# Cross-attention on one core: the next pair's queries and first keys ahead of the last product with the values, denominators and output moved later

## The reference

```python
# x: (2, 256, 256), ctx: (2, 4096, 256), 16 heads of 64
q = (layernorm(x) @ w_q); k = ctx @ w_k; v = ctx @ w_v      # split into heads
attn = softmax(q @ k^T * 64 ** -0.5)                          # (2, 16, 256, 4096)
x = x + (attn @ v, heads side by side) @ w_o
```

## Time and profile before

| | |
|---|---|
| median of 3 runs | 1456.81 us (1455.27 to 1457.78) |
| profiled execution | 1455.65 us |
| its span, first to last instruction | 1453.9 us, mean granted clock 0.964 |
| TensorE busy | 1299.6 us, 89% |
| VectorE busy | 983.6 us, 68% |
| ScalarE busy | 877.8 us, 60% |
| GpSimd busy | 245.4 us, 17% |
| first queries projected (L518) to last output (L606) | 25.8 to 1167.3 us |

### The profile page before, as it was taken

The page is one execution under the profiler, slowest core; times in us unless marked ns, Lnnn a source line. Parts: engine busy times, 40 slices in busy tenths (PEclk is TensorE's granted clock), DMA queues, the critical chain, the costliest instruction groups (busy, mean ns, idle before and its releaser), DMA issues. The chain is left out here.

```text
span 1453.9 us, 22869 instructions
## 1 busy us (share of the span) xinstructions
PE 1299.6 (89%) x8447; PEld 1003.3 (69%) x8447; DVE 983.6 (68%) x1256; ACT 877.8 (60%) x1562; POOL 245.4 (17%) x245
## 2 busy tenths in 40 slices
PE   4999999999999999899999999999999969887643
PEld 3877787868687878697768687877777733666322
DVE  4657676777767687656777767685858555735476
ACT  5758585857676676565767676675757412534152
POOL 4202021211212120111211212020303022020000
PEclk9999999999999999999999999999999979998776
DMA  4000000000000001200000000000000054261000
GB/s 163 1 1 19 1 19 9 12 19 1 19 1 15 1 19 55 80 1 13 7 19 1 20 1 19 1 20 1 15 1 5 1 169 64 27 80 16 22 0 15
DMA packets 29684, 34.70 MB, mean 24 GB/s; under 512 B 3984, under 2 KB 26000, under 8 KB 29328
## 3 DMA queue, kind: packets, MB, share of 16 engines
q1 hardware_dynamic: 27536, 29.83, 8.0%
q0 software_dynamic: 2048, 3.43, 1.7%
HBM read 25.89 MB, written 0.52 MB: 18 GB/s over the span
## 5 line engine op out<-in xcount | busy, mean ns | idle before, releaser
L463 DVE TENSOR_TENSOR prob_sum<-prob_sum,probs 128x1024 f32<-128x1024 f32 x224 | 264.5, 1222 | 164.6 <-ACT probs L382 163.9
L382 ACT ACTIVATE probs<-scores_a 128x1024 f32<-128x1024 f32 x128 | 131.2, 1025 | 209.1 <-PE scores_a L578 208.1
L315 POOL TENSOR_TENSOR k_split<-prob_sum,k_split 64x512 fp32r<-64x512 f32 x128 | 165.0, 1289 | 303.2 <-ACT prob_sum L358 303.2
L442 DVE TENSOR_REDUCE step_max<-scores_a 128x2 f32<-128x1024 f32 x128 | 156.9, 1225 | 37.3 <-PE scores_a L566 35.5
L442 DVE TENSOR_REDUCE step_max<-scores_b 128x2 f32<-128x1024 f32 x128 | 155.7, 1216 | 0.0
L577 PE MATMUL scores_a<-q_twice,k_split 128*128 128x256 f32 x512 | 139.1, 305 | 5.0 <-ACT q_low_max L373 4.9
L308 POOL TENSOR_TENSOR w_lo<-w_raw,w_hi 128x768 fp32r<-128x768 f32 x16 | 34.9, 2181 | 593.8 <-ACT w_hi L327 593.7
L382 ACT ACTIVATE probs<-scores_b 128x1024 f32<-128x1024 f32 x128 | 131.3, 1026 | 0.0
L577 PE MATMUL scores_b<-q_twice,k_split 128*128 128x256 f32 x512 | 128.4, 283 | 0.0
L578 PE MATMUL scores_b<-q_low_max,k_ones 128*128 128x256 f32 x512 | 127.9, 282 | 0.0
L578 PE MATMUL scores_a<-q_low_max,k_ones 128*128 128x256 f32 x512 | 127.9, 283 | 0.0
(11 more groups left out here) (214 smaller groups left out, 2641.3 us busy)
## 6 DMA issues: line engine op xcount, KB each, us to landing
ctx_rows<-in_ctx_dram SPq DMA_DIRECT2D x10, 512.0 KB, 3.6
w_raw<-in_L_xattn_w_v_dram SPq DMA_DIRECT2D x14, 256.0 KB, 3.2
probs<-in_ctx_dram SPq DMA_DIRECT2D x6, 512.0 KB, 6.1
grouped<-dots_sb SPq DMA_DIRECT2D x16, 136.0 KB
grouped<-dots_sb POOLq DMA_DIRECT2D x16, 136.0 KB, 13.2
w_raw<-in_L_xattn_w_q_dram SPq DMA_DIRECT2D x16, 128.0 KB, 2.3
w_raw<-in_L_xattn_w_k_dram SPq DMA_DIRECT2D x16, 128.0 KB, 2.4
wo_pair<-in_L_xattn_w_o_dram SPq DMA_DIRECT2D x16, 128.0 KB, 2.1
```

What stands on the lines that cost most here:

```text
L315: pool.tensor_tensor(k_split[0:DH, B, keys], k_staged_b[j % 2], k_split[DH:P, B, keys].bitcast(F32), ALU.subtract).then_inc(k_low[B], 1)
L382: act.activation(probs[:, j % 2, h, :], flat_scores[h], ACT.Exp, scale=SCALE).then_inc(exp_done, 1)
L442: dve.tensor_reduce(step_max[:, :, 1 - h, j - 1], scores[h][:, :, :], X, ALU.max).then_inc(max_done, 1)
L463: dve.tensor_tensor(prob_sum[:, h, :], prob_sum[:, h, :], probs[:, j % 2, h, :], ALU.add).then_inc(sum_done, 1)
```

## The change

The program of each engine keeps its operations but gets another order around the boundary of two pairs.

- TensorE: within a batch, `project_q` and `project_k` of step 0 of the *next* pair are issued before the last `product_with_v` of this one. In the next pair, `sum_over_keys` comes behind `project_k` of step 1, `project_output` behind the first `scores_for_max` at step 2. For the first pair of a batch `sum_over_keys` comes behind `project_k` of step 0.
- ScalarE: `split_weights` for the next pair behind the exponentials of step 3; the copies of the next queries and of the high keys of step 0 at the end of the pair; the staged copies of steps 0 and 1 wait for `den_made`.
- VectorE: `divide` moves behind the correction of keys 1 (L435 at j = 1), `add_output` from j = 1 to behind `low_queries` at j = 2.
- The hardware loop covers four pairs of a batch, not six; pairs 5 to 7 are written out.

```diff
@@ -215,11 +215,12 @@
 
 
             body(b * PAIRS, b, 0, 0)
-            with eng.Fori(0, PAIRS // 2 - 1) as k:
+            with eng.Fori(0, PAIRS // 2 - 2) as k:
                 for parity in (1, 0):
                     i = k * 2 + (2 - parity)
                     body(b * PAIRS + i, b, i, parity)
-            body((b + 1) * PAIRS - 1, b, PAIRS - 1, 1)
+            for i in range(PAIRS - 3, PAIRS):
+                body(b * PAIRS + i, b, i, i % 2)
 
         def context_banks(n):
 
@@ -247,6 +248,9 @@
 
         def is_first(it):
             return isinstance(it, int) and it == 0
+
+        def stays_in_batch(i):
+            return not (isinstance(i, int) and i == PAIRS - 1)
 
         def last_batch(b, i):
 
@@ -337,25 +341,38 @@
                     own = v_near[:, tiles, :] if half == parity else v_far[:, half, tiles, :]
                     act.activation(own, src[:, :, 0:PAIR], ACT.Copy).then_inc(v_copied, 1)
 
-            def body(it, b, i, parity):
-                if not is_first(it):
-                    split_weights(it, b, i)
-
+            def high_queries(it):
                 act.wait_ge(q_made, it + 1)
                 for h in (A, B):
                     for half in (0, DH):
                         act.activation(q_twice[half:half + DH, h, :], v_ps[h * DH:(h + 1) * DH, 0:SEQ],
                                        ACT.Copy).then_inc(q_high, 1)
+
+            def high_keys(it, j):
+                keys = slice(j * CHUNK, (j + 1) * CHUNK)
+                act.wait_ge(k_made, STEPS * it + j + 1)
+                ps = k_ps[j % 2]
+                act.activation(k_split[0:DH, A, keys], ps[0:DH, :], ACT.Copy).then_inc(k_high, 1)
+                act.activation(k_split[DH:P, B, keys], ps[DH:P, :], ACT.Copy).then_inc(k_high, 1)
+
+            def stage_keys(it, j):
+                if j >= 2:
+                    act.wait_ge(k_low[B], STEPS * it + j - 1)
+                else:
+                    wait_past(act, den_made, it)
+                act.activation(k_staged_b[j % 2], k_ps[j % 2][DH:P, :], ACT.Copy).then_inc(k_staged, 1)
+
+            def body(it, b, i, parity):
+                if is_first(i):
+                    if b > 0:
+                        split_weights(it, b, i)
+                    high_queries(it)
                 for j in range(STEPS + 1):
                     if j < STEPS:
                         keys = slice(j * CHUNK, (j + 1) * CHUNK)
-                        act.wait_ge(k_made, STEPS * it + j + 1)
-                        ps = k_ps[j % 2]
-                        act.activation(k_split[0:DH, A, keys], ps[0:DH, :], ACT.Copy).then_inc(k_high, 1)
-                        act.activation(k_split[DH:P, B, keys], ps[DH:P, :], ACT.Copy).then_inc(k_high, 1)
-                        if j >= 2:
-                            act.wait_ge(k_low[B], STEPS * it + j - 1)
-                        act.activation(k_staged_b[j % 2], ps[DH:P, :], ACT.Copy).then_inc(k_staged, 1)
+                        if j > 0 or is_first(i):
+                            high_keys(it, j)
+                        stage_keys(it, j)
                     if j > 0:
 
                         keys = slice((j - 1) * CHUNK, j * CHUNK)
@@ -383,8 +400,13 @@
                                        ).then_inc(exp_done, 1)
                     if j == 0:
                         copy_v(b, i, parity, STEPS - 1)
+                    if j == 3 and stays_in_batch(i):
+                        split_weights(it + 1, b, i + 1)
                     if next_group(b, i, j) is not None:
                         context_high(act, next_group(b, i, j))
+                if stays_in_batch(i):
+                    high_queries(it + 1)
+                    high_keys(it + 1, 0)
                 if next_group(b, i, STEPS) is not None:
                     context_high(act, next_group(b, i, STEPS))
             for b in range(BATCH):
@@ -424,8 +446,6 @@
                                       ALU.subtract).then_inc(q_low, 1)
                     dve.tensor_tensor(q_low_max[DH:P, B, :], v_ps[DH:P, 0:SEQ], q_twice[DH:P, B, :].bitcast(F32),
                                       ALU.subtract).then_inc(q_low, 1)
-                if not is_first(it):
-                    divide(it - 1)
                 for j in range(STEPS + 1):
                     if j < STEPS:
                         keys = slice(j * CHUNK, (j + 1) * CHUNK)
@@ -435,7 +455,7 @@
                         dve.tensor_tensor(k_split[DH:P, A, keys], ps[0:DH, :], k_split[0:DH, A, keys].bitcast(F32),
                                           ALU.subtract).then_inc(k_low[A], 1)
                     if j == 1 and not is_first(it):
-                        add_output(it - 1, last_batch(b, i))
+                        divide(it - 1)
                     if j > 0:
                         for h in (A, B):
                             dve.wait_ge(pre_made, 2 * (STEPS * it + j - 1) + h + 1)
@@ -443,6 +463,8 @@
                                               ).then_inc(max_done, 1)
                     if j == 2:
                         low_queries()
+                        if not is_first(it):
+                            add_output(it - 1, last_batch(b, i))
                 dve.wait_ge(max_done, 2 * STEPS * (it + 1))
                 dve.tensor_reduce(row_max[:, :, :], step_max[:, :, :, :], X, ALU.max).then_inc(max_chain, 1)
                 dve.wait_ge(max_chain, 2 * it + 1)
@@ -608,10 +630,8 @@
                 last.then_inc(y_made, 1)
 
             def body(it, b, i, parity):
-                project_q(it, b)
-                if not is_first(it):
-                    sum_over_keys(it - 1)
-                pe.wait_ge(w_low, it + 1)
+                if is_first(i):
+                    project_q(it, b)
                 for j in range(STEPS):
                     if j >= 2:
 
@@ -619,14 +639,20 @@
                         pe.wait_ge(k_staged, STEPS * it + j - 1)
                     if is_first(i):
 
+                        pe.wait_ge(w_low, it + 1)
                         pe.wait_ge(ctx_low, DC * (j + 1 if b == 0 else (b + 1) * LOADS))
-                    project_k(it, j)
-                    if j == 1 and not is_first(it):
-                        project_output(it - 1)
+                    if j > 0 or is_first(i):
+                        project_k(it, j)
+                    if j == (0 if is_first(i) else 1) and not is_first(it):
+                        sum_over_keys(it - 1)
                     if j == 2 and is_first(i):
                         pe.wait_ge(ctx_low, DC * (b + 1) * LOADS)
                     if j > 1:
+                        if j == 2:
+                            pe.wait_ge(q_high, 4 * it + 4)
                         scores_for_max(it, j - 2)
+                    if j == 2 and not is_first(it):
+                        project_output(it - 1)
                     if j > 3:
                         project_v(it, b, i, parity, j - 4)
                 scores_for_max(it, STEPS - 2)
@@ -657,6 +683,10 @@
                         product_with_v(it, b, i, parity, j - 1)
                     if next_group(b, i, j) is not None:
                         transpose_context(next_group(b, i, j))
+                if stays_in_batch(i):
+                    project_q(it + 1, b)
+                    pe.wait_ge(w_low, it + 2)
+                    project_k(it + 1, 0)
                 product_with_v(it, b, i, parity, STEPS - 1)
                 if next_group(b, i, STEPS) is not None:
                     transpose_context(next_group(b, i, STEPS))
```

## The result

| | before | changed |
|---|---|---|
| median of 4 runs | 1456.93 us | 1472.84 us (1472.3 to 1474.54) |
| profiled execution, its span | 1455.65, 1453.9 us | 1472.59, 1470.8 us |

The change makes the kernel slower: ratio 1.0113, 95% interval 1.0095 to 1.013. The spans differ by 16.9 us.

A forecast was written before the change was run, and what follows sets the result against it. A pair's end hangs on its first product for the values, behind VectorE's chain and the addition, despite TensorE's 89% busy. Ordinary boundaries 8.4, jumps 4.4, batch boundary 1.2: +14.0 on 1455.65, so 1470 us; range 1457 to 1477.

The forecast's parts named there:

- The chain: Pair boundary: denominators, staged copy, high keys 1, correction, division, first maximum, with the addition still to come before v(0).
- den_made later: Ordinary boundary: the denominators come 1.2 us later, behind the next pair's queries and keys on TensorE.
- First maximum: VectorE's first row maximum after an ordinary boundary starts at 460.65 instead of 460.88, 0.2 us sooner.
- v(0) and the ordinary boundary: First product for the values waits for the late output addition; net +0.7 us a boundary, bounds +0.4 to +1.1.
- Rule of v(0) plus a constant: A pair ends a constant time after its first product for the values, which hangs on VectorE's chain and y_added.
- The jump: Loop's jump back, one a batch, falls between product 7 and keys 1: +1.5 us each, bounds 0 and 2.2.
- Batch boundary: Pair 7 to 8: keys 0 ahead of the denominators make the first product for the values 1.2 us later.
- Exponentials: Stretch of exponentials: moving split_weights and w_lo there costs 0, at worst 1.5 us a pair.
- rival 3: Contention in the exponentials: w_lo's 1.5 us of blocking stops them, 21 us on top, 1491; chance 0.03.
- moved with w_lo: The fold ends some 1.5 us sooner, but that time goes to a running sum in e-step 3 or 4.
- Rival 1: TensorE is the bound and gets its idle time back at the fold: 21 us faster, 1435; chance 0.11.
- Rivals 2 and 4: First: late addition hidden, only jumps cost, 1457, chance 0.11. Second, counted within it: fold's wait and denominators swap places, 1456.

The follow-up runs named there:

- 2: Changed kernel with the division moved ahead of the correction of keys 1 on VectorE; 1452.83 us, ratio 0.9991.
- 3: Changed kernel with staged copies and reciprocal in columns of prob_sum that the denominators' product does not read; 1457.21 us, ratio 1.0015.
- experiment 1: Changed kernel with add_output ahead of low_queries at step 2 on VectorE; 1469.01 us, ratio 1.0106.
- experiment 7: Kernel before with only split_weights for the next pair moved behind the exponentials of step 3; 1439.58 us, ratio 0.9897.

## Why the prediction was right, point by point

- **Direction, mechanism and size.** Predicted 1470 and slower by 14 us, measured 1472.84 and slower by 15.9. That the two are so close is in part luck: the sum's own terms, the boundaries, came to 19.8 in the traces, and 2.9 us went off outside the pairs. The chain was the one described, and two experiments that break it at different links (2 and 3) each give 1.2 us a boundary back.
- **den_made later.** Predicted 1.2 us later than before, measured 1.49 (6.54 against 5.05). The rest lies in the rows between product 6 and the denominators (455.86 to 463.66 where written out): four blocks each 0.04 to 0.14 longer than booked, 0.3 in all. The prediction's bounds had such an amount, as switches between shapes; no run separates the cause.
- **First maximum.** Predicted 0.2 sooner, measured 0.14 in the loop and 0.0 where written out.
- **v(0) and the ordinary boundary.** Predicted +0.7 for both. Measured +0.85 at v(0) in the loop and +1.0 where written out, +0.8 in the mean of 12 periods.
- **Rule of v(0) plus a constant.** True for the change (v(0)→end 20.01 against 20.05), false as a rule: experiment 1. Removing y_added's wait brings v(0) 0.89 sooner and wins 0.25.
- **The jump.** This term was mis-sized: 1.5 each, measured 3.3 and 2.2 at the denominators, 7.4 in place of 4.4 in the sum. The price was taken from one jump of the kernel before, where TensorE waits 1.3 to 1.8 us at the four jumps; here it waits 2.10 and 2.17, and at one jump the clock fell on top. Why the wait is longer in the new order is open.
- **Batch boundary.** exp→v(0) +1.3, predicted +1.2; the period rose by 2.7, because the stretch of exponentials of pair 7 took 1.3 more. The stretch waits for context transposes and took 35.7 to 37.3 in all the kernels here, so that part is not shown to belong to the change.
- **Exponentials.** Cost 0, right (31.41 against 31.42); rival 3 is out, by experiment 7 too. But the price of w_lo was not "moved with w_lo" to a running sum, as the prediction has it: no running sum got longer, and the fold's 1.5 us were saved.
- **What the prediction overlooked.** It booked w_lo's move as worthless, since in the new order the fold is not waited for. It is right for the sum, but the same move was worth 17 us in the old order. The change spends it: against kernel 7, which has only this part, the rest of the change costs 2.3 us an ordinary boundary.
- **The signs.** Those named came: the staged copy waits 2.64 us for the denominators, the reciprocal starts 0.72 after the correction, v(0) waits 0.71 for the addition, the fold takes 1.22. The first maximum starts 12.6 us after product 6, not under 11.8.
- **Rival 1** (TensorE gets its idle time back) falls: L598's wait went, and three others of 2.4 us came. **Rivals 2 and 4** (a wash) fall too: the ordinary boundaries, which have no jump, are 0.8 us longer each.

## What to carry to other kernels

Where an engine waits for another at a boundary, look first at what delays the other one there; here the fold was slow only because an unrelated instruction of GpSimd ran beside it, and moving that alone won 17 us, while all the rest, in the best order found, won under 5 more. When work is pulled ahead of a producer, list what now waits for that producer and what is queued behind each waiting instruction: one copy placed in a shared buffer held up two other engines. A jump back is free only under somebody else's wait; check what it will stand in after a reordering.

## What the runs showed of the hardware

- The first step of the fold (a VectorE addition of 128x1024) takes 1.22 us alone and 2.71 beside GpSimd's w_lo, in 14 of 16 pairs; moved apart, 1.22 in all 16. w_lo itself takes 1.80 alone and up to 2.28 beside VectorE's sums. The Trainium skill (SBUF — State Buffer, Who interferes with whom) says that a VectorE instruction with two SBUF inputs contends with a GpSimd instruction that reads SBUF; the traces agree.
- At a jump back TensorE had nothing to issue for 1.3 to 1.8 us in the kernel before and for 1.6 to 2.2 in the changed kernel and its variants. After one such pause of 2.1 us the granted clock fell to about the lower level (0.53), after another of 2.17 in the same execution it did not (1.00).
- Written out bodies reach the first exponential 0.3 us sooner after the last transpose of the maxima (L644, L670) than bodies in the loop (2.59 against 2.91), in every kernel here, the first and last pair of a batch apart. Why is open; no run separates it.
